# Moving an expert mixture's gates from matrix products to DMA in a fused attention-and-experts block

## What is computed

```python
x = x + conv(ln(x))                     # shifted 7 x 7 window attention, 4 heads of 8 channels
t = x as tokens
t = t + ffn(ln(t))                      # top-2 of 8 experts, each 32 -> 32

# attention, per window of 49 tokens and per head
attn = softmax(q @ k.T) + bias + mask   # bias and mask are added AFTER the softmax
out  = (attn @ v) @ w_proj + b_proj

# experts, per token
p = softmax(t @ router_w + router_b); top_p, top_i = top_k(p, 2); top_p /= sum(top_p)
y = sum_k top_p[k] * (t @ expert_w[top_i[k]] + expert_b[top_i[k]])
```

## Time and profile before

| | us |
|---|---|
| median of 3 runs | 838.19 |
| lowest and highest | 836.32, 843.77 |
| the profiled execution | 836.74 |
| its span, first to last instruction | 834.9 |
| PE, DVE, ACT, POOL busy in the span | 676.2, 547.7, 386.1, 486.1 |

### The profile page before, as it was taken

One profiled execution on the slowest core, in us unless ns is written; L12 is line 12 of the kernel. 1 busy time (PEld: TensorE's weight loads), 2 busy tenths in 40 slices (PEclk: granted clock), 3 DMA queues, 4 the chain that ended last, 5 costly groups with the idle time before them and its releaser, 6 DMA issues.

```text
span 834.9 us, 29295 instructions
## 1 busy us (share of the span) xinstructions
PE 676.2 (81%) x12514; PEld 443.7 (53%) x12514; DVE 547.7 (66%) x999; ACT 386.1 (46%) x705; POOL 486.1 (58%) x539
## 2 busy tenths in 40 slices
PE   0787879888887879889797988888898988878666
PEld 0465555655556556546565554555656655645331
DVE  6242657768586767678676667857676767766443
ACT  1645464646364455626464463635355563622110
POOL 4616676575757666664757566574766666541520
PEclk9979989999999999988989889999999999997555
DMA  4100221413231131413231131323223230403040
GB/s 128 30 3 3 57 62 41 90 50 79 61 79 50 32 79 47 93 41 79 60 80 50 28 84 41 79 59 69 51 50 70 54 86 22 88 13 79 20 97 19
DMA packets 19008, 48.11 MB, mean 58 GB/s; under 512 B 9536, under 2 KB 9536, under 8 KB 17344
## 3 DMA queue, kind: packets, MB, share of 16 engines
q1 hardware_dynamic: 18448, 45.06, 23.3%
q10 hardware_dynamic: 432, 1.19, 0.4%
HBM read 7.69 MB, written 6.42 MB: 17 GB/s over the span
## 4 chain that ended last, share of the span: by engine, by line
PE 45%; DVE 32%; issue 11%; ACT 6%; POOL 4%; DMA 0%; SPq 0%; DVEq 0%; ACTq 0%; POOLq 0%
DVE mx L866 9%; PE ps_shared L1119 6%; PE ps_win L1190 6%; PE ps_acc L1287 5%; PE ps_pv L1205 5%; PE ps_shared L1143 4%; PE ps_weight L1273 4%; PE ps_win L1161 4%; PE ps_shared L1228 3%; DVE zt L979 3%; DVE x L979 3%; DVE x L907 2%; PE ps_win L1184 2%; DVE ms L880 2%; ACT ot L754 2%
## 5 line engine op out<-in xcount | busy, mean ns | idle before, releaser
L866 DVE TENSOR_REDUCE mx<-ps_win 128x32 f32<-128x1568 f32 x64 | 114.5, 1789 | 64.6 <-PE ps_win L1161 64.1
L979 DVE TENSOR_TENSOR zt<-ps_weight,x 128x392 f32<-128x392 f32 x118 | 66.1, 561 | 89.5 <-PE ps_weight L1273 89.0
L776 ACT ACTIVATE pt<-ps_win 128x784 f32<-128x784 f32 x128 | 98.4, 821 | 44.0 <-PE ps_win L1190 43.6
L1273 PE MATMUL ps_weight<-wt,const_bf_tile 96*128 96x392 bf16 x234 | 84.1, 359 | 41.1 <-DVE zt L979 20.7
L611 POOL TENSOR_TENSOR on<-on,obs 128x256 f32<-128x256 f32 x64 | 46.6, 729 | 120.0 <-DVE on L893 92.6
L1205 PEld LDWEIGHTS ps_pv<-vb,pt 128*49 128x49 f32 x4096 | 104.9, 129 | 15.3 <-issue 13.0
L1205 PE MATMUL ps_pv<-vb,pt 128*49 128x18 f32 x4096 | 109.7, 201 | 0.0
L979 DVE TENSOR_TENSOR x<-ps_weight,x 128x392 f32<-128x392 f32 x116 | 65.4, 564 | 38.3 <-PE ps_weight L1273 36.9
L766 ACT COPY mr<-ps_win 128x512 bf16<-128x512 bf16 x64 | 37.5, 587 | 95.8 <-PE ps_win L1169 95.8
L1190 PE MATMUL ps_win<-qbd,kp 32*49 32x196 f32 x2048 | 79.0, 370 | 0.0
L590 POOL TENSOR_TENSOR st<-st,minus_half 112x28 f32<-112x28 f32 x16 | 77.0, 4812 | 1.3
(11 more groups left out here) (134 smaller groups left out, 1318.8 us busy)
## 6 DMA issues: line engine op xcount, KB each, us to landing
x<-x SPq DMA_DIRECT2D x48, 392.0 KB, 5.1
x_kept<-xin SPq DMA_DIRECT2D x16, 392.0 KB, 3.4
x<-x2t SPq DMA_DIRECT2D x64, 98.0 KB, 2.2
xin<-x SPq DMA_DIRECT2D x32, 150.0 KB
out<-xo SPq DMA_DIRECT2D x32, 150.0 KB
xin<-x SPq DMA_DIRECT2D x32, 18.0 KB
out<-xo SPq DMA_DIRECT2D x32, 18.0 KB
weight_tile<-weights ACTq DMA_DIRECT2D x1, 560.0 KB, 4.6
```

The source lines that it names most:

```text
L776: nc.scalar.activation(pt[g % 2][:, k, :, :, :].rearrange("p a h n -> p a (h n)"), ps_win[:, :, HN * k:HN * k + HN], ACT.Exp).then_inc(pro ...
L866: nc.vector.tensor_reduce(mx[g % 2].rearrange("n a x h -> n a (x h)"), ps_win[:, :, 0:8 * N].rearrange("n a (k m) -> n a k m", m=N), AX, A ...
L979: nc.vector.tensor_tensor(tokens if eh else zt[:, a, :], weight_bank(w, 1 + i)[:, 0:HALF], tokens, ALU.mult).then_inc(weight_drained, 1)
L1273: mm(weight_bank(w, 1 + i)[:, 0:HALF], weight_sel[:, eh, a, :], wt[:, HALF * half:HALF * half + HALF], start=True, stop=True).then_inc(wei ...
```

## The change

The change rewrites the mixing, the norms' roots, the shared banks and the order of a step:

- **Gates by DMA.** The top-2 weights stay float32. PE turns them (`share`), ACT copies them to `shares`, SP stores these to a tensor in DRAM in 4 DMAs, waits for them, and reads every expert's rows back in 8 DMAs that repeat each row over 32 partitions (`gate_rows`). Each of the 8 fills 32 partitions x 4 x 784 float32, 401 KB. The split, the 16 products and `ps_weight` go.
- **Gated tokens.** DVE multiplies `gates` with `x4`, both in SBUF, in 4 instructions of 4 x 448 or 4 x 336 columns (`mul`).
- **Second shared bank.** All fills of `ps_shared` alternate between two banks; a fill waits until the last but one is drained (`shared_free`).
- **Router turned.** 4 products of 32 rows and 2 transposes instead of 7 products; ACT drains them; top 2 now works on 98 x 256 instead of 112 x 224.
- **64x64 projections.** q and k are each made by 4 products on 64 x 64 quarters of the array, both halves of the unit at once (`project`), instead of 2 products of 128 x 128.
- **Roots.** The power is replaced by a logarithm and an exponential on ACT, and three small DVE instructions (a Newton step). The projection's bias is added to `x_kept` by GpSimd (`kept`) instead of by a product.
- **Half of `kmask`** moves from ACT to GpSimd.
- **The order of a step** is new (`SIDE_TASKS`, `PROLOGUE`, `TAIL`). `att`, `ahead`, `next_unit`, `post` and `older` mean the same as before.

```diff
 SIDE_TASKS = {
-    (0, 0): [("ot", 1), ("keep", 0), ("wt", 0), ("y", 0), ("mix", 0), ("back", 0), ("mix", 1), ("y", 1), ("back", 1), ("norm2_center", 0)],
-    (0, 1): [("xt", 0), ("mix", 2)],
-    (0, 2): [],
-    (0, 3): [("mix", 3), ("norm2_square", 0), ("xt", 1), ("mix", 4), ("norm2_scale", 0)],
-    (1, 0): [("qk", 0), ("load", 0), ("mix", 5)],
-    (1, 1): [("qk", 1), ("mix", 6)],
-    (1, 2): [],
-    (1, 3): [("mix", 7), ("qk", 2)],
-    (2, 0): [("mix", 8), ("x2t", 0), ("norm1_center", 0), ("mix", 9)],
...
+    (0, 0): [("norm1_root", 0), ("top2", 3), ("top2", 4), ("keep", 0), ("ot", 1), ("xt", 0), ("xt", 1), ("top2", 5)],
+    (0, 1): [("load", 0), ("y", 0)],
+    (0, 2): [("back", 0), ("share", 0), ("q", 0), ("y", 1)],
+    (0, 3): [("back", 1), ("gates", 0), ("norm2_center", 0)],
+    (1, 0): [("k", 0), ("norm1_center", 0)],
+    (1, 1): [("norm2_square", 0)],
+    (1, 2): [("v", 0), ("place", 0), ("norm2_scale", 0)],
+    (1, 3): [("kept", 0), ("norm2_root", 0)],
+    (2, 0): [("kmask", 0), ("norm1_square", 0), ("mul", 0)],
+    (2, 1): [("x2t", 0)],
+    (2, 2): [("x2t", 1), ("norm1_scale", 0), ("mul", 1), ("sum", 0)],
+    (2, 3): [("route", 0), ("replicate", 0), ("mul", 2)],
+    (3, 0): [("v", 1), ("logits", 0), ("sum", 1), ("mix_drain", 0), ("kmask", 1), ("top2", 0)],
+    (3, 1): [("place", 1), ("sum", 2)],
+    (3, 2): [("ob", 0), ("top2", 1), ("mul", 3)],
+    (3, 3): [("ob", 1), ("sum", 3), ("top2", 2), ("mix_drain", 1), ("top2_exp", 0), ("ot", 0), ("final", 0), ("final", 1), ("store", 0)],
 }
...
+            def gate_rows(w, _):
+
+                sp.wait_ge(shares_drained, upto("shares_drained", w))
+                if w.has_before(1):
+                    sp.wait_ge(gates_low, upto("gates_low", w.before(1)))
+                    sp.wait_ge(gates_high, upto("gates_high", w.before(1)))
+                for b in range(4):
+                    sp.dma_start(shares_kept[:, BLOCK * b:BLOCK * b + BLOCK],
+                                 shares[32 * b:32 * b + 32, :]).then_inc(shares_stored, 16)
+                sp.wait_ge(shares_stored, upto("shares_stored", w))
+                if w.has_before(1):
+                    sp.wait_ge(mixed, upto("mixed", w.before(1)))
+                for eh in range(2):
+                    for e in range(4):
+                        rows = bass.AP(shares_kept.tensor, shares_kept.offset + (4 * eh + e) * COLS,
+                                       [[0, C], [E * COLS, A], [1, COLS]])
+                        sp.dma_start(gates[C * e:C * e + C, eh, :, :], rows).then_inc(gates_high if eh else gates_low, 16)
...
+            def norm1_scale(v, _):
+
+                act.wait_ge(sqsum1, upto("sqsum1", v))
+                nc.scalar.activation(st1[:, 1, :], st1[:, 2, :], ACT.Ln, bias=eps1[:, 0:1]).then_inc(log1, 1)
...
+                nc.scalar.activation(st1[:, 3, :], st1[:, 1, :], ACT.Exp, scale=-0.5, bias=guess_scale[:, 0:1]).then_inc(guess1, 1)
...
-                tokens = x4[w.par][:, a, HALF * half:HALF * half + HALF]
-                nc.vector.tensor_tensor(tokens if eh else zt[:, a, :], weight_bank(w, 1 + i)[:, 0:HALF], tokens,
-                                        ALU.mult).then_inc(weight_drained, 1)
+            def mul(w, i):
+
+                eh, half = divmod(i, 2)
+                dve.wait_ge(x4_ready, upto("x4_ready", w))
+                if eh:
+                    dve.wait_ge(gates_high, upto("gates_high", w))
+                else:
+                    dve.wait_ge(gates_low, upto("gates_low", w))
+                gate = gates[:, eh, :, columns(half)]
+                nc.vector.tensor_tensor(gate, gate, x4[w.par][:, :, columns(half)], ALU.mult).then_inc(gated, 1)
...
+            def project(name, w64, v):
...
+                for b in range(2):
+                    for r in range(2):
+                        rows, to = slice(64 * r, 64 * r + 64), 64 * (r ^ b)
+                        ins = mm(halves[b][to:to + 64, 0:HALF], w64[rows, rows],
+                                 xt[rows, 8 * b:8 * b + 8, :, :].rearrange("p q k i -> p (q k i)"), start=True, stop=True)
+                    ins.then_inc(pre_filled, 1)
```

More of the change, by code:

```diff
@@ L166, in macro_step, with program @@
         yield from side((g, 3))
-def program(eng):
-    unit = [fixed(n) for n in range(UNITS)] + [None, None]
+def program():
+    unit = [None, None] + [Unit(n) for n in range(UNITS)] + [None, None]
     seen = []
@@ L543, in _ @@
                     replicate(unit, i)
+                elif step == "gates":
+                    gate_rows(unit, i)
                 elif step == "store":
@@ L667, in _ @@
                     place(unit, i)
-                elif step == "top2" and i >= 5:
+                elif step == "kmask" and i == 1:
+                    kmask(unit, i)
+                elif step == "kept":
+                    kept(unit, i)
+                elif step == "top2" and i == 5:
                     top2(unit, i)
@@ L716, in kmask, with k_drain @@
+            def k_drain(v, _):
+                for half in range(2):
+                    act.wait_ge(pre_filled, upto("pre_filled", v, 4 + half))
+                    if v.has_before(2):
+                        act.wait_ge(scores_filled, upto("scores_filled", v.before(2)))
+                    nc.scalar.copy(kp[v.par][:, 8 * half:8 * half + 8, :],
+                                   shared("k", v, 0, half)[:, 0:HALF].rearrange("p (q n) -> p q n", n=N)).then_inc(pre_drained, 1)
             def kmask(v, i):
-                act.wait_ge(pre_drained, upto("pre_drained", v, 3 + 2 * i))
+                act.wait_ge(pre_drained, upto("pre_drained", v, 4 + i))
@@ L805, in _ @@
             act.dma_start(const_bf16_tile[:, :], consts_bf16).then_inc(weights_loaded, 16)
-            for step, unit, i in program(act):
+            for step, unit, i in program():
                 if step == "norm1_square":
@@ L810, in _ @@
                     norm2_square(unit, i)
+                elif step == "norm1_scale":
+                    norm1_scale(unit, i)
                 elif step == "prepare" and unit.number == 0:
@@ L814, in _ @@
                     xt_drain(unit, i)
-                elif step == "qk":
-                    qk_drain(unit, i)
-                elif step == "kmask":
+                elif step == "q":
+                    q_drain(unit, i)
+                elif step == "k":
+                    k_drain(unit, i)
+                elif step == "kmask" and i == 0:
                     kmask(unit, i)
@@ L1043, in _ @@
             ones(vb[0])
-            for step, unit, i in program(dve):
+            for step, unit, i in program():
                 if step == "norm1_center":
@@ L1048, in _ @@
                     norm1_scale(unit, i)
+                elif step == "norm1_root":
+                    norm1_root(unit, i)
                 elif step == "norm2_center":
@@ L1052, in _ @@
                     norm2_scale(unit, i)
+                elif step == "norm2_root":
+                    norm2_root(unit, i)
                 elif step == "prepare" and unit.number == 0:
@@ L1076, in _ @@
             mm = nc.tensor.matmul
-            def shared_free(name, u, i):
-                at = SHARED_ORDER.index((name, i))
-                for back in range(1, 2 * len(SHARED_ORDER)):
-                    lap, k = divmod(at - back, len(SHARED_ORDER))
-                    before, j = SHARED_ORDER[k]
-                    w = u.moved(lap - later(name, i) + later(before, j))
-                    if w is not None:
-                        kind, first = SHARED_BANK[before]
-                        drained = {"pre": pre_drained, "ot": ot_drained, "token": token_drained}[kind]
-                        pe.wait_ge(drained, upto(f"{kind}_drained", w, first + j))
-                        return
@@ L1298, in _ @@
             mm(ps_acc[:, 0:FOLDED], part["centre"], part["raw"], start=True, stop=True).then_inc(centred_weights, 1)
-            for step, unit, i in program(pe):
+            for step, unit, i in program():
                 if step == "xt":
@@ L1323, in _ @@
                     x2t_turn(unit, i)
[L1324 to L1329 removed]
+                elif step == "route":
+                    route(unit, i)
+                elif step == "logits":
+                    logits_turn(unit, i)
+                elif step == "share":
+                    share_turn(unit, i)
+                elif step == "sum":
+                    experts(unit, i)
                 elif step == "final":
```

581 lines of the change are left out of this document (289 added, 292 removed), and 16 rows, old and new, of tables (PROLOGUE, SIDE_TASKS, TAIL, per_unit).

## The result

The changed kernel takes **993.59 us** in the median of 4 runs (989.8 to 994.43), the kernel before beside it 837.26. The ratio is 1.184, with a 95% interval of 1.177 to 1.192. The forecast was 952, the range 895 to 1,010. The profiled execution has a span of 992.6 us and a mean granted clock of 0.753, where it was 0.908.

A forecast was written before the change was run, and what follows sets the result against it. No engine is full: each 46.5 us step is four 7.4 us loops plus waiting for side tasks, mostly PE's. Forecast: 34 + 34 + 50 + 12 x 56.2 + 46.5 + 32 = 871, tail 79, span 950, plus 2: 952 us; range 895 to 1,010.

The forecast's parts named there:

- The first wait: Group 1: VectorE's sum waits for `xin`, loaded 10.1 us after the residual, and stands still 9 us in every step.
- the first rival: Whole kernel: `xin` and gates are there when VectorE comes; a step takes 45.8 us, 813 us in all; chance 0.06.
- The second wait: VectorE's multiplications wait for gate DMAs: low gates 22.2 us after the residual, high ones 7.5 us later.
- Group 2, 12.8: Group 2 of a step takes 12.8 us, its maximum behind the 2.05 us multiplication by low gates arriving at 34.0.
- The rival that costs only the load's wait: Gate transfers run faster than the copies, so multiplications don't wait: step 52.9 us, 912 us in all; chance 0.13.
- a rival of its own: Clock and shadow: half the path's products at half speed and shadows on the path; step 61, 1,010 us; chance 0.10.
- GpSimd's shadow: All four multiplications read SBUF and meet busy GpSimd: 1.3 us a step, 0.25 counted, at worst 12 us in total.
- step 0: First step, with neither residual nor gates: 34 us; its group 0 starts at 34 instead of 38.1, one power less.
- the tail: After the last exponentials: 79 us instead of 69.9, since gates of units 14 and 15 come one after the other.
- The projection's quarters: PE: four quarters run together, about halving projection time; otherwise 0.8 us on group 0's path, 10 us in all.
- the reads are not slow: Slow reads rival: 32 partitions read one DRAM row at half the rate; step 72 us, 1,140 us; chance 0.04.
- the removals: Powers, spreading products and projection time taken off GpSimd and PE: cover, not time; alone 45.8 us a step against 46.5.

The follow-up runs named there:

- the later sum: Changed kernel with VectorE's sum over the loaded unit `xin` and GpSimd's centring one group later, in group 2: 990.77 us, ratio 1.202.
- the three kept buffers: Changed kernel with three buffers of `x_kept` instead of two, so `keep` waits for the residual of three units back: 922.07 us, ratio 1.122.
- the kernel before with the sum moved: Kernel before with VectorE's sum over the loaded unit one group earlier, ahead of group 2's maximum: 856.9 us, ratio 1.021.
- an eighth of the gates: Changed kernel with the eight gate DMAs moving an eighth of their columns, the other gates set once by a memset: 999.58 us, ratio 1.212.
- both edits: Changed kernel with the sum over `xin` one group later and gate DMAs of an eighth of their columns: 920.57 us, ratio 1.104.
- the idle products: Unread extra PE products in group 1: 12 in the changed kernel, 996.52 us; 10 in the three-buffer, reordered, eighth-gates kernel, 874.5 us.
- the kernel with both waits shortened: Changed kernel with three `x_kept` buffers, reordered top 2, norm 1's root and norm 2's scaling, gate DMAs of an eighth: 880.34 us, ratio 1.051.

## Why the forecast was right, and where its sizes were off

**The first wait: right in place and size.** `xin` was to come 10.1 us after the residual and came 9.2 after it (549.14 to 558.33); VectorE was to stand still for 9 us and did for 8.1, with 9.3 the longest. Group 1 was forecast at 16.4 and averages 16.2. The term is confirmed by the later sum (group 1 at 10.0, where the first rival has 9.3), by the three kept buffers (10.1), and by the kernel before with the sum moved.

**The second wait: right in time, wrong in what it costs.** The low gates were forecast 22.2 us after the residual; the multiplication could start at 20.5. The bulk of that data moved at 223 GB/s (window 561 to 569, DMA share 1.02), where I took 201 from the earlier trace rows. The Trainium skill's 341 GB/s (DMA: Bandwidth & Descriptors, section Bandwidth, Measured) was not reached by this form of transfer. The step of the prediction that failed is "Group 2, 12.8: VectorE would be free, but the multiplication by the low gates (...) stands ahead of the maximum". The length is right, 12.4 on average, but by luck: removing the gates' wait won nothing. The rival that costs only the load's wait rests on the same step. It gave 912 if the gates come in time. They did come in time in the experiment with an eighth of the gates, and the time was 999.58. PE's stream at the 1.2 GHz level and GpSimd's chain of bias addition and scaling end group 2 just as late. I had walked group 2 with durations taken at full clock. So the two waits together were priced too high: 10.4 us a step in the forecast (56.2 against the first rival's 45.8), while shortening both gave 5.1 (the step at 52.8 with both edits) and 5.8 (three buffers).

**The clock: underrated.** I gave it a rival of its own and nothing in the sum. In group 2 it costs 3.0 us (12.5 against 9.5), of which 0.9 are lost again in group 3, so it was inside the 12.8 us that I attributed to the gates. That PE's idle stretch in group 1 is its cause is not shown. In the changed kernel the idle products left group 2 at 0.51 to 0.61, and in the kernel with both waits shortened they raised it in 6 of 12 steady steps. In the kernel before, the granted clock of group 2 fell to 0.77 in the step of the earlier trace rows, behind a group 1 of 7.7 us in which PE had been busy throughout.

**GpSimd's shadow: in the direction forecast, larger.** I counted 0.25 us of 1.3. In the step above, VectorE's 0.54 us instruction took 2.57 and ended with GpSimd's bias for `x_kept`, as in 5 of the 12 full steps. It is the last of the three of norm 2's root, forecast at 0.19 each: they take 0.39, 0.53 and 0.54 in the median, those of norm 1's, of the same form, 0.18 to 0.19. In the step above GpSimd was at work beside all three.

```profile
565.84 2.07 POOL L640 TENSOR_TENSOR x_kept<-x_kept,weight_tile 112x896 f32<-112x896 f32 x1
568.03 1.70 POOL L584 TENSOR_TENSOR xc<-xc,st 112x896 f32<-112x896 f32 x1
574.84 2.96 POOL L601 TENSOR_TENSOR on<-on,obs 128x256 f32<-128x256 f32 x1 [5.11 <-DVE on L970]
```

The last row is the other way round: GpSimd's sum for `on`, 0.73 us on average in the kernel before (1.22 now), took 2.96 beside a multiplication of 1.55, once in each full step. Nothing that ran here takes this apart from the rest, so its share of the time stays open.

**The sum, term by term.** Measured against forecast: up to the first exponentials 34.8 against 34; step 0 42.5 against 34; step 1 53.3 against 50; steps 2 to 13 together 694.8 against 674.4; step 14 49.4 against 46.5; step 15 35.0 against 32; the tail 82.7 against 79. The span is 992.6 instead of 949.9. Half of the 43 us lie in the full steps, mostly in groups 0 (13.3 against 12.3) and 3 (16.0 against 14.7). 8.5 lie in step 0, which I shortened below the 38.2 us of before on account of cover that was never on its path. The projection's quarters did run together (0.89 us for both halves of q), and the high gates' multiplication waited less than the first (0.30 us), as forecast; the reads are not slow.

**Where the time went, as far as shown.** Of 156 us over the kernel before, the two waits with the order of groups 0 and 3 make 113 (993.59 to 880.34; the two waits alone 73), with 27.8 us of waiting for `xin` still left. The lower clock in group 2 makes some 26 more, 12 steps of 2.2 us, an estimate from the two full-clock steps against the usual one shown. 5 are the memset, which the changed kernel doesn't have. That leaves about 12 open, and the wait for `xin` behind the stores is a part of them that nothing here prices. My first rival, 813 with all transfers in time, was tested by the same kernel, as near as these runs come to it, and came out 67 us too low. Its steps 2 to 13 take 49.5 us instead of 45.8, 44 us in all, more than half of it the clock's by the same estimate; 16 more lie ahead of step 2, 5 of them the memset. With group 2 at full clock the step was 46.9, no better than the 47.1 that the kernel before averages over steps 2 to 13: the removals won nothing, as forecast.

## What to carry to other kernels

When a table moves an instruction ahead of another, ask which transfer it waits for and how late that lands, since one group made some 18 us here in a kernel that had no wait at all. When two waits end within a few microseconds of each other, removing one shows nothing; price them by removing both, and read from the list of waits whether they are gone. When one wait of a queue is taken away, look what stands next in that queue. Before trusting a walk through a stage that will stand idle, redo it with PE's durations at the lower clock.

## What the runs showed that I had not expected

The granted clock has a rhythm in the step, not just a level. In the kernel with both waits shortened, a steady step reads 0.81, 0.85, 0.50 and 1.00 over its four groups, and the lower clock itself keeps PE busy: 11.10 of 12.6 us in group 2, where 6.46 of 9.5 do the same work at full clock. A busy share is therefore no measure of work here. The 3.42 us of a GpSimd scaling that takes 1.70 alone, beside a VectorE multiplication with both operands in SBUF, show the wait from GpSimd's side; in the earlier trace rows it was VectorE that waited.
